# Attention scores from two scaled f16 parts, two heads in the halves of TensorE's rows, and row maxima without a mask operand

## The reference

```python
qkv = x @ W_qkv.T                                    # q, k, v: 16 heads of 16
scores = einsum('bhqd,bhkd->bhqk', q, k) / sqrt(16)  # 1024 x 1024 a head
scores = where(tril, scores, -inf)
attn = softmax(scores, axis=-1)
out = einsum('bhqk,bhkd->bhqd', attn, v)
x = layernorm(x + out @ W_proj.T)
h = silu(x @ wg.T) * (x @ wu.T)                      # weights int / 127
x = layernorm(x + h @ wd.T)
```

## Time and profile before

| | |
|---|---|
| median of 3 runs | 1554.4 us |
| span of the profiled execution | 1558.1 us |
| PE busy | 1467.7 us (94%) |
| DVE busy | 1208.7 us (78%) |
| ACT busy | 940.5 us (60%) |
| POOL busy | 353.7 us (23%) |
| moved by DMA | 140.58 MB, mean 90 GB/s |

### The profile page before, as it was taken

How to read it: one execution, slowest core, us unless ns; L and a number is a source line. 1 busy time by engine, 2 the same in 40 slices (tenths; PEclk the granted TensorE clock), 3 DMA queues, 4 the chain that set the end, 5 groups by cost and what they waited for, 6 DMA issues and landing times.

```text
span 1558.1 us, 34187 instructions
## 1 busy us (share of the span) xinstructions
PE 1467.7 (94%) x9300; PEld 689.1 (44%) x9300; DVE 1208.7 (78%) x3122; ACT 940.5 (60%) x2055; POOL 353.7 (23%) x436
## 2 busy tenths in 40 slices
PE   8999969999998998998998998999898999999997
PEld 5665523333333333333333333333333666666664
DVE  4555577897897987987997987998762777887776
ACT  3545415776776775776776776777576444444443
POOL 5000001211211221221121121122121443444434
PEclk9999967999998999999999999999899999999999
DMA  7777993575475466457447547546401022212211
GB/s 246 229 238 229 232 138 42 72 86 67 62 90 73 56 83 85 57 74 90 61 66 91 67 57 92 71 61 110 65 13 38 28 81 81 69 52 81 81 55 41
DMA packets 173313, 140.58 MB, mean 90 GB/s; under 512 B 80208, under 2 KB 148304, under 8 KB 173136
## 3 DMA queue, kind: packets, MB, share of 16 engines
q1 hardware_dynamic: 173136, 138.46, 48.7%
HBM read 87.29 MB, written 50.33 MB: 88 GB/s over the span
## 4 chain that ended last, share of the span: by engine, by line
PE 83%; issue 6%; DVE 6%; DMA 3%; ACT 2%; SPq 0%; DVEq 0%; POOL 0%; POOLq 0%; ACTq 0%
PE ps L1180 18%; PE ps L1109 15%; PE ps L1092 14%; PE ps L1238 11%; PE ps L1055 7%; PE ps L1253 4%; PE ps L1151 4%; PE ps L1062 4%; DVE ps L841 3%; PE ps L1199 3%; DMA q_stack<-max_rows 1%; DVE row_max L841 1%; PE ps L1223 1%; PE ps L1044 1%; ACT x_hi_rows L738 1%
## 5 line engine op out<-in xcount | busy, mean ns | idle before, releaser
L841 DVE CUSTOM_DVE_ANT_0 ps<-ps,causal 128x1024 f32<-128x1024 f32 (+7 forms) x1024 | 746.1, 790 | 129.1 <-PE ps L1092 125.1
L700 ACT ACTIVATE probs<-ps 128x512 f32<-128x512 f32 (+3 forms) x1536 | 653.7, 495 | 274.4 <-PE ps L1109 265.6
L1109 PE MATMUL ps<-q_stack,k_stack 99*128 99x512 bf16 (+3 forms) x1536 | 402.7, 334 | 39.2 <-issue 19.5
L1092 PE MATMUL ps<-k_stack,q_stack 96*128 96x512 bf16 (+3 forms) x1536 | 361.8, 338 | 13.4 <-DVE row_max L841 5.9
L589 POOL TENSOR_SCALAR_AFFINE_SELECT probs<-probs 128x512 f32<-128x512 f32 x256 | 162.5, 635 | 806.8 <-ACT probs L700 806.8
L1180 PE MATMUL ps<-probs,v_ones 128*32 128x512 f32 (+3 forms) x3072 | 335.3, 509 | 0.5 <-POOL probs L589 0.5
L1109 PEld LDWEIGHTS ps<-q_stack,k_stack 99*128 99x128 bf16 x1536 | 132.8, 98 | 266.5 <-ACT probs L700 143.5
L1092 PEld LDWEIGHTS ps<-k_stack,q_stack 96*128 96x128 bf16 x1536 | 135.1, 99 | 187.5 <-DVE row_max L841 51.4
L619 POOL TENSOR_TENSOR h_lo<-h_sb,h_hi 128x512 f16<-128x512 f32 x96 | 119.3, 1248 | 197.9 <-ACT h_hi L757 197.9
L841 DVE DVE_READ_ACCUMULATOR2_ANT row_max<- 128x1 f32 x1024 | 145.9, 142 | 0.0
L749 ACT ACTIVATE silu<-ps 128x512 f32<-128x512 f32 x96 | 57.3, 597 | 127.5 <-PE ps L1238 127.5
(11 more groups left out here) (89 smaller groups left out, 1272.8 us busy)
## 6 DMA issues: line engine op xcount, KB each, us to landing
qk_parts<-parts SPq DMA_DIRECT2D x64, 384.0 KB, 2.8
q_stack<-qk_parts SPq DMA_DIRECT2D x192, 128.0 KB, 6.9
k_stack<-qk_parts SPq DMA_DIRECT2D x192, 128.0 KB, 7.3
x_sb<-in_L_attn_x SPq DMA_DIRECT2D x32, 512.0 KB, 4.5
v_rows<-v_sb SPq DMA_DIRECT2D x16, 512.0 KB, 3.2
v_flat<-v_rows SPq DMA_DIRECT2D x32, 256.0 KB, 10.8
attn_rows<-attn_sb SPq DMA_DIRECT2D x64, 128.0 KB, 2.1
v_sb<-attn_rows SPq DMA_DIRECT2D x16, 512.0 KB, 5.5
```

Source lines behind the costliest of these rows:

```text
L700: act.activation(probs[s % RING][:, j, 0:w], ps[:, 4 + n % 3, 0:w], ACT.Exp, scale=SOFT_SCALE).then_inc(exp_done, 1)
L841: last = dve.tensor_tensor_reduce(scores, scores, causal[:, T - w:T], 1.0, LOWEST, ALU.add, ALU.max, row_max[:, j * QT + qt:j * QT + qt + 1])
L1092: last = pe.matmul(ps[:, 2 * pair + c0 // CH, c0 % CH:c0 % CH + w], q_stack[g][0:ROWS, j, tile_cols(qt)], k_stack[g][0:ROWS, j, k0:k0 + w] ...
L1109: pe.matmul(ps[:, 4 + n % 3, 0:w * P], k_stack[g][0:ROWS_M, j, tile_cols(kt)], q_stack[g][0:ROWS_M, j, q0:q0 + w * P], start=True, stop=Tr ...
```

## The change

Queries and keys are now two f16 parts instead of three bf16 parts. Before they are split, they are scaled by powers of two: DVE takes the largest magnitude of the query weights, of the key weights and of x chunk by chunk, POOL reduces these over the partitions (`partition_all_reduce`, once for the weights and once a batch), and DVE makes the scales from the exponent bits (`scales`). ACT writes the high part with the scale applied, DVE the low part in one instruction; the second pair of passes is gone. The exponential on ACT takes its scale from a register, which is loaded once a batch. x has four buffers instead of two. The chunks of the projections are written out instead of looped, on all four engines.

A stack holds three blocks of 16 rows a head (high by high, high by low, low by high) and two rows for the maxima: 50 rows. Two heads of a group lie in rows 0 to 49 and two in rows 64 to 113, and a stack tile has two columns of heads instead of four. A stack is loaded by 12 DMAs of 64 KB. The rows of maxima take four DMAs instead of three; the key stack's constant rows come by eight small DMAs ahead of attention.

A unit of maxima is one query tile by up to 512 keys for two heads at once, head 0 of the pair in bank 0 of the pair of banks and head 1 in bank 1, 24 units a group. On the diagonal four short matmuls add the mask (`one_of_half` by `above`) to the scores. DVE takes the two maxima in one `tensor_reduce` over PSUM, without a mask operand. The two halves of long rows are joined in `split_max`, which then makes two parts in two instructions. The planner's costs are changed, and `UNITS_AHEAD` is 16.

The core of the diff (left out are the buffers, semaphores, the wait values that follow from the counts, and the same unrolling on other engines):

```diff
-    COLS, EXP, ROW_MAX, PV, TURN = 54, (50, 107), (68, 134), (110, 214), 428
-    MASK, COPY, COPY_ROWS, NORMALISE, SPLIT = 594, 478, 158, 650, 950
+    COLS, EXP, ROW_MAX, PV, TURN = 54, (60, 107), (150, 134), (150, 214), 428
+    PAIRED, ABOVE = 0.55, 90
+    MASK, COPY, COPY_ROWS, NORMALISE, SPLIT = 594, 478, 158, 650, 650
     PE_ACT, PE_DVE, ACT_PE, DVE_PE, ACT_POOL, POOL_PE = 240, 330, 150, 230, 230, 180
...
-    PAIRS = [(0, 0), (1, 0), (2, 0), (0, 1), (1, 1), (0, 2)]
+    HI, LO = 0, 1
+    PAIRS = [(HI, HI), (HI, LO), (LO, HI)]
     ROWS = len(PAIRS) * DH
-    ROWS_M = ROWS + 3
+    ROWS_M = ROWS + 2
+    SIDE = 64
+    MAX_UNIT = 2.0 ** 15
+    TINY = 2.0 ** -40
+    EXPONENT = 0x7F800000
...
-    for j in range(0, HG, 2):
-        for k in (j, j + 1):
-            max_units += [[(k, QT - 1)]] + [[(k, QT - 1 - t), (k, t - 1)] for t in range(1, QT // 2)]
-        max_units.append([(j, QT // 2 - 1), (j + 1, QT // 2 - 1)])
+    for p in range(HG // 2):
+        for qt in range(QT - 1, QT // 2 - 1, -1):
+            max_units += [(p, qt, 0), (p, QT - 1 - qt, 0), (p, qt, 1)]
     NU = len(max_units)
-    UNITS_AHEAD = 12
...
+            def load_stacks(b, g, blocks=range(len(PAIRS))):
+
+                for r in blocks:
                     pair = PAIRS[r]
                     for which, stack in ((0, q_stack), (1, k_stack)):
                         src = qk_dram[which, pair[which], g * HG * DH:(g + 1) * HG * DH, bass.ds(b * T, T)]
-                        sp.dma_start(stack[g][r * DH:(r + 1) * DH, :, :],
-                                     src.rearrange("(j r) t -> r j t", j=HG)).then_inc(stack_loaded[g], 16)
+                        by_side = src.rearrange("(p i r) t -> i r p t", p=HG // 2, i=2)
+                        for i in range(2):
+                            row = i * SIDE + r * DH
+                            sp.dma_start(stack[g][row:row + DH, :, :], by_side[i]).then_inc(stack_loaded[g], 16)
 
             def load_v(b, g):
                 sp.dma_start(v_flat[g % 2][:], v_tiles[:, bass.ds(b * QT, QT), g * HG * DH:(g + 1) * HG * DH]
...
             def load_max_rows(g):
-                for part in range(3):
-                    sp.dma_start(q_stack[g][ROWS + part:ROWS + part + 1, :, :].rearrange("p j (t c) -> p (j t) c", c=P),
-                                 max_rows[part * NM:(part + 1) * NM, :]).then_inc(max_rows_loaded, 16)
+                for part in range(2):
+                    for i in range(2):
+                        row = i * SIDE + ROWS + part
+                        sp.dma_start(q_stack[g][row:row + 1, :, :].rearrange("r p (t c) -> r (p t) c", c=P),
+                                     max_rows[part * NM + i * HG // 2 * QT:part * NM + (i + 1) * HG // 2 * QT, :]
+                                     ).then_inc(max_rows_loaded, 16)
...
+            sp.wait_ge(preset, 4)
+            for g in range(4):
+                for i in range(2):
+                    row = i * SIDE + ROWS
+                    sp.dma_start(k_stack[g][row:row + 2, :, :], unit_rows[:]).then_inc(unit_rows_loaded, 16)
             for par in range(2):
                 load_stacks(0, 0, range(par, len(PAIRS), 2))
-                chunk_a(2 * PAIRS_LOOPED + par, PAIRS_LOOPED, par, False)
...
+
+            def share_x_max(b):
+                pool.wait_ge(x_max_done, 2 * b + 2)
+                pool.partition_all_reduce(x_max_all[:, 2 * b:2 * b + 2], x_max[:, 2 * b:2 * b + 2], P,
+                                          bass.bass_isa.ReduceOp.max).then_inc(x_max_shared, 1)
+
+            pool.wait_ge(w_max_done, 2)
+            pool.partition_all_reduce(w_max_all[:], w_max[:], P, bass.bass_isa.ReduceOp.max).then_inc(w_max_shared, 1)
+            share_x_max(0)
+            share_x_max(1)
             for k, (name, n_, b_) in enumerate((("gate", wgate_n, wgate_b), ("up", wup_n, wup_b),
                                                 ("down", wdown_n, wdown_b))):
+            for b in range(2, B):
+                share_x_max(b)
             for i in range(2):
...
+            def part_hi(c, m):
                 act.wait_ge(qk_ready, 4 * c + m + 1)
                 act.wait_ge(parts_stored[m], 16 * c + 16)
-                act.copy(parts[m][:, 0, :], ps[:, 2 + m, :]).then_inc(part0_done, 1)
-
-            def part1(c, m):
...
-                part0(c, 3)
-                part1(c, 2)
-                part1(c, 3)
+                act.activation(parts[m][:, HI, :], ps[:, 2 + m, :], ACT.Copy,
+                               scale=qk_scale[:, c // 2, m // 2:m // 2 + 1]).then_inc(part_hi_done, 1)
+
+            def chunk_a(c):
+                if c + 1 < NCH:
...
-                               scale=SOFT_SCALE).then_inc(exp_done, 1)
-
+                               scale=scale_of_batch).then_inc(exp_done, 1)
+
+            scale_of_batch = act.alloc_register("scale_of_batch")
+            act.wait_ge(scale_ready, B)
+            act.reg_load(scale_of_batch, exp_scale[0:1, 0:1].bitcast(I32))
             for n in range(HG * AHEAD):
...
         def _(dve):
+            dve.wait_ge(w_loaded["qkv"], 16)
+            for which in range(2):
+                dve.tensor_reduce(w_max[:, which:which + 1], wqkv_n[:, 2 * which:2 * which + 2, :], AX.XY, ALU.max,
+                                  apply_absolute_value=True).then_inc(w_max_done, 1)
+
+            def x_maximum(c):
+                dve.wait_ge(x_loaded[c % 4], 16 * (c // 4) + 16)
+                dve.tensor_reduce(x_max[:, c:c + 1], x_sb[c % 4][:], AX.XY, ALU.max,
+                                  apply_absolute_value=True).then_inc(x_max_done, 1)
+
+            x_maximum(0)
+            x_maximum(1)
             for u in range(1, len(early_units), 2):
...
-            def rest_of(c, m):
-                dve.wait_ge(part0_done, 4 * c + m + 1)
-                dve.wait_ge(part1_done, 4 * c + m + 1)
-                dve.wait_ge(part2_done, 4 * c + m + 1)
-                dve.tensor_tensor(rest[m % 2][:], ps[:, 2 + m, :], parts[m][:, 0, :],
-                                  ALU.subtract).then_inc(qk_bank_free, 1)
-
-            def part2(c, m):
-                dve.wait_ge(part1_done, 4 * c + 2 + m + 1)
-                dve.tensor_tensor(parts[m][:, 2, :], rest[m % 2][:], parts[m][:, 1, :],
-                                  ALU.subtract).then_inc(part2_done, 1)
...
+            def scales(b):
+                dve.wait_ge(x_max_shared, b + 1)
+                dve.scalar_tensor_tensor(out=x_bound[:, b:b + 1], in0=x_max_all[:, 2 * b:2 * b + 1], scalar=TINY,
+                                         in1=x_max_all[:, 2 * b + 1:2 * b + 2], op0=ALU.max,
+                                         op1=ALU.max).then_inc(scale_step, 1)
+                dve.wait_ge(scale_step, 3 * b + 1)
+                power_and_inverse(x_power[:, b:b + 1], x_scale[:, b:b + 1], x_bound[:, b:b + 1], scale_step)
+                dve.wait_ge(scale_step, 3 * b + 3)
+                dve.tensor_scalar(qk_scale[:, b, :], w_scale[:], x_scale[:, b:b + 1], None, ALU.mult)
+                dve.scalar_tensor_tensor(out=exp_scale[:, b:b + 1], in0=x_power[:, b:b + 1], scalar=w_power_qk[:],
+                                         in1=x_power[:, b:b + 1], op0=ALU.mult, op1=ALU.mult).then_inc(scale_ready, 1)
+
+            def part_lo(c, m):
+                dve.wait_ge(part_hi_done, 4 * c + m + 1)
+                dve.scalar_tensor_tensor(out=parts[m][:, LO, :], in0=ps[:, 2 + m, :],
+                                         scalar=qk_scale[:, c // 2, m // 2:m // 2 + 1], in1=parts[m][:, HI, :],
+                                         op0=ALU.mult, op1=ALU.subtract).then_inc(qk_bank_free, 1)
+
...
+                if c % 2 == 0 and c + 2 < NCH:
+                    x_maximum(c + 2)
+                    x_maximum(c + 3)
+                if c % 2 and c + 1 < NCH:
+                    scales(c // 2 + 1)
...
+            copy_xt(0)
+            dve.wait_ge(w_max_shared, 1)
+            scales(0)
+            for c in range(NCH):
+                chunk_a(c)
...
-                k0 = 0
-                for j, qt in max_units[u % NU]:
-                    w = (qt + 1) * P
-                    scores = ps[:, 2 * pair:2 * pair + 2, :].rearrange("p a b -> p (a b)")[:, k0:k0 + w]
-                    last = dve.tensor_tensor_reduce(scores, scores, causal[:, T - w:T], 1.0, LOWEST, ALU.add, ALU.max,
-                                                    row_max[:, j * QT + qt:j * QT + qt + 1])
-                    k0 += w
-                last.then_inc(s_free, 1)
+                p, qt, half = max_units[u % NU]
+                w = min(CH, (qt + 1) * P - half * CH)
+                dve.tensor_reduce(row_max[:, half, :, p, qt], ps[:, 2 * pair:2 * pair + 2, 0:w], AX.X,
+                                  ALU.max).then_inc(s_free, 1)
...
-                dve.tensor_copy(max_parts[:, 0, :], row_max[:]).then_inc(max_step, 1)
-                dve.wait_ge(max_step, 4 * count + 1)
```

(45 more changed lines are left out.)

233 lines of the change are left out of this document (127 added, 106 removed).

## The result

The changed kernel takes **1665.0 us** (median of 4 runs, 1654.9 to 1674.5) against 1554.3 for the kernel before: ratio 1.072, 95% interval 1.066 to 1.078. The forecast was 1473 us, faster. The profiled execution spans 1670.7 us, 112.6 more than before.

The account below looks back on a forecast made before the run. PE was taken to bound attention, 27.5 of 28.4 us a group. 1558.1 - 84 (loop) - 2 (first maxima) + 6 (start) - 1 (last group) = 1477 us span, 1473 as median; range 1422 to 1525.

Parts of the forecast that it names:

- PE's work: Attention, per group: maxima, mask, scores, value steps, turns and shape changes sum to 23.8 us on PE.
- Rival 3: Attention: the two row halves do not run together; PE 30.7 us, period 31.7, time 1650 us; chance 0.09.
- DVE's work: Attention, per group: reductions 21.2, split 0.7, normalisations 1.4, together 23.3 us on DVE.
- The period: Attention, one group: 2.4 us for eight short or half units on DVE's 23.3, taken as 26.0 us.
- the rest of the loop: Attention loop outside the 31 periods: batch boundaries 45 us and 2 us left of a wait.
- ACT: Attention: the same 48 exponentials a group, 20.4 us busy, with 6 us of slack.
- Rival 4 (the clock): Attention: a quarter of PE's work at 1.2 GHz; PE 29.8 us, period 30.8, time 1622 us; chance 0.05.
- Rival 2 (starving, 27.4): Attention: PE and DVE starve each other over short units and value steps; period 27.4, time 1516 us; chance 0.17.
- the start of the projections: Before the projections: PE's first turn of x starts at 12.5 us, not 9.56; +3 us, ends 0 and +12.
- reductions across partitions: Start, on POOL: two reductions that no row shows; at 1 to 3.5 us each they would be hidden.
- the first maxima: Stretch from 194.5 to 218.9 us, DVE-bound: falls to 22.7 us, -2.
- The wait of 11.4 us: Loop, rows of the first maxima behind stack loads: at half the bytes 2 us of it is left.

Follow-up runs that it names:

- packed version: The changed kernel with its short maxima units sharing banks two by two, 18 units a group instead of 24, in a newly planned order: 1514.8 us.
- experiment 11: The packed version with both heads of a maxima unit, and the mask's matmuls, in rows 0 to 47, one behind the other: 1655.5 us.
- experiments 1 and 2: 1 is the packed version, 1514.8 us; 2 is its written order with the shared units split again into 24 a group, 1589.7 us.
- the price: The changed kernel with the planner's cost of scores put back from 0.55 to a whole matmul, only the order changing: 1562.8 us.
- packing: The packed version with the planner's price of scores at a whole matmul: 1505.7 us.
- the latencies: The packed version with the price at a whole matmul and planner latencies PE to ACT 300, back 180 ns, for 240 and 150: 1476.9 us.
- experiment 2: The packed version's written order with its shared units split again, each with its own pair of banks, 24 a group: 1589.7 us.
- version of 1476.9 us: The packed version with the planner's price at a whole matmul and its PE-ACT latencies at 300 and 180 ns: ratio 0.950.

## Why the prediction was wrong

**PE's work: right in its sum.** The forecast had 23.8 us a group. In the packed version the times by which PE is over 150 ns late against its columns at full clock, start to start, add up to 4.1 us an interval: 27.6 - 4.1 = 23.5. The terms were not each measured. Rival 3 is out (0.22 us a pair, and experiment 11). The page "TensorE: Matmul & The Clock Gate" of the Trainium skill (Measured speedup vs the span model) has packed tiles some 4 ns apart; the trace agrees, with starts of mostly 3 to 4 ns apart where nothing stands between.

**DVE's work: right.** 23.3 us were forecast, 23.56 are busy. A 2x512 reduction takes 1.13 us start to start, priced at 1.14; the missing accumulator read bought nothing, as assumed.

**The period: wrong, the step that failed.** It put 2.4 us on 23.3 ("Eight short or half units at 0.3") and took 26.0; measured is 32.8, 6.8 more. Over 31 intervals that is 210 us; the rest of the loop came to 33 us where 47 were forecast, and the two make the miss of 196 us in the loop. The step priced only DVE running dry behind a short unit. It missed three things:
- Short units tie up a pair of banks each: 2.5 us a group (experiments 1 and 2) for the 2.4 given them. The size was right, but it comes on top of a packed period of 27.6, not of DVE's 23.3, and what waits is PE for its banks.
- The order. The forecast took the planner's order as even, though the diff gave the planner a new price and new costs. Where five units stand in a row at the group's end, PE waits for DVE. The order from that price cost 3.8 us (32.8 to 29.0), of which the clock is some 1.7.
- ACT. The forecast left it out as 20.4 us of work in a longer period. Halving the exponentials gives 2.4 us in the packed version; that it is latency is likely and not shown.

These overlap and are not a sum, but the steps on one way down are. From 32.8, the price gives 3.8 (29.0), packing 1.4 (27.6) and the latencies 1.1 (26.45).

That this lies near 26.0 is luck. The forecast's 26.0 was for split units; by its own reasoning packed ones would be back near PE's 23.8 and DVE's 23.3, and 26.45 is over 2.5 us more. The loop of 854.0 is 31 x 26.45 and 34, where the forecast had 31 x 26.0 and 47.

**Rival 4 (the clock), given 0.05.** It happened: 7.0 of 32.8 us are at half clock, 21%, near the quarter supposed. "Against: ... a slow PE is again a busy one" was no protection: after the bunch the clock falls in most groups. But I priced it at 4.8 us an interval and it costs 1.7, probably because part of the slow time is time in which PE would have waited. Its 1622 us, 43 under the result, is two errors that partly cancel: the clock priced too high, the rest left out.

**Rival 2 (starving, 27.4), given 0.17.** Right in kind, 5.4 us an interval too small.

**The sums.** The working takes +3 us for the start of the projections, the last sum has +6: by the terms as worked out the forecast is 1470, not 1473. Rival 3 would decide at 27.5 us of PE, which is over half of the way from 23.8 to its 30.7, not a third. Neither changes the account.

**The other terms** hardly matter. PE's first turn of x and the first reductions across partitions:

```profile
10.70 3.84 PE L1126 MATMUL ps<-ident,x_sb 128*128 128x128 f32 x16 [2.06 <-DVE wqkv_t L840]
...
13.20 0.37 POOL L610 PARTITION_ALL_REDUCE w_max_all<-w_max  x1 [8.75 <-issue]
...
13.48 0.43 POOL L606 PARTITION_ALL_REDUCE x_max_all<-x_max  x1
```

The turn starts at 10.70, not 12.5, 1.1 later than before, and the loop starts no later for it. The reductions across partitions take 0.4 us in the records (times on POOL are rough), under the low end of my 1 to 3.5, and hide. DVE's busy time in the first maxima fell from 23.59 to 21.67 us, but the stretch did not: 24.6 long, 24.4 before, where -2 was forecast. The wait of 11.4 us is gone, as forecast: the first interval went from 40.6 to 33.1 us.

## What to carry to other kernels

When a change makes one engine's pieces shorter and uneven, price the number of handshakes and the buffers that each piece holds, not only the work, and pack short pieces until each fills its buffer. Where a program writes the order of the work from costs, those costs are part of the change: read the written order for stretches in which one engine's queue holds only one kind of work, and try several. A margin of 3 us between the two busiest engines' work (before) is worth keeping; with PE and DVE level and ACT's round trip likely close behind, work saved turned into waits.

## What was not expected of the hardware

In these traces TensorE's mean clock isn't told by its busy time. From 600 to 960 us the kernel before and experiment 11 have the same busy time. The kernel before:

```profile
600.00:960.00 360.00, 343.80 (x2428) 128.96 (x2426) 310.75 (x881) 258.17 (x617) 68.24 (x109) 0.99 0.57 73
```

Experiment 11:

```profile
600.00:960.00 360.00, 344.08 (x2870) 144.51 (x2869) 258.50 (x338) 229.41 (x554) 61.69 (x99) 0.89 0.18 43
```

343.8 and 344.1 us of 360, at clocks of 0.99 and 0.89. The second has some of that busy time because its clock is low. Its matmuls for maxima and mask use half of the rows, one behind the other; whether that matters to the clock was not tried. The changed kernel and experiment 2 in the same stretch are busy for 304 and 300 us, at 0.87 and 0.97. "TensorE: Matmul & The Clock Gate" of the Trainium skill (What's actually happening) has the clock follow how busy PE has been recently; a mean busy share, as these rows show, can't tell it.

This is a change from the halves to a value step, in PE's timeline of the version of 1476.9 us:

```profile
688.12 0.38 PE L1200 MATMUL ps<-q_stack,k_stack 50*128 50x512 f16 x1
688.75 0.39 PE L1200 MATMUL ps<-q_stack,k_stack 50*128 50x512 f16 x1 [0.25 <-ACT probs L747]
689.07 1.06 PE L1271 MATMUL ps<-probs,v_ones 128*32 128x512 f32 x8
```

688.75 to 689.07 is 0.32 where a matmul of this size takes 0.22 before another of its kind: the change costs 0.10 us, as the 0.09 of the earlier trace rows from full height.
